# Four-stage sequence model on one core: the turned scores' mask moves from TensorE to VectorE, and two loads of constants move ahead

## Time and profile before

| | |
|---|---|
| median of 3 runs | 4013.48 us (4013.28 to 4015.05) |
| profiled execution | 4030.09 us, its span 4028.3 us |
| busy shares of the span | PE 85%, PEld 58%, DVE 70%, ACT 47%, POOL 22% |
| mean granted clock | 0.936 |
| stage A | about 30 to 899 us of the span |
| stage B begins | 899 us; stage C begins 1785 us |

### The profile page before, as it was taken

The page is one execution under the profiler, slowest core; times in us unless marked ns, Lnnn a source line. Parts: engine busy times, 40 slices in busy tenths (PEclk is TensorE's granted clock), DMA queues, the critical chain, the costliest instruction groups (busy, mean ns, idle before and its releaser), DMA issues.

```text
span 4028.3 us, 71096 instructions
## 1 busy us (share of the span) xinstructions
PE 3416.4 (85%) x28530; PEld 2342.5 (58%) x28530; DVE 2804.6 (70%) x5487; ACT 1889.0 (47%) x3121; POOL 868.1 (22%) x908
## 2 busy tenths in 40 slices
PE   6999999987489888856888888888888888869995
PEld 4555555553255555534566666666666666748774
DVE  4666566555588889856767777777777777647775
ACT  3444444335378787824334444444444443226662
POOL 4000000003312122221122222222222221215553
PEclk7989899898699999978999999999999999969997
DMA  8999300000343434220000000000000000026666
GB/s 293 394 394 372 47 1 2 1 21 24 129 147 119 142 126 137 70 67 1 1 6 7 7 7 7 7 6 7 5 5 7 5 6 7 12 83 230 217 219 184
DMA packets 161497, 354.43 MB, mean 88 GB/s; under 512 B 13821, under 2 KB 98559, under 8 KB 154768
## 3 DMA queue, kind: packets, MB, share of 16 engines
q1 hardware_dynamic: 147088, 324.44, 23.5%
q0 software_dynamic: 14080, 25.45, 1.9%
HBM read 136.82 MB, written 216.67 MB: 88 GB/s over the span
## 4 chain that ended last, share of the span: by engine, by line
PE 54%; DVE 26%; ACT 10%; issue 5%; DMA 2%; SPq 1%; POOL 1%; another core or an unknown queue 0%; DVEq 0%; POOLq 0%; ACTq 0%
DVE t L2185 6%; PE ps L1583 5%; PE ps L134 4%; PE ps L1641 4%; PE ps L136 3%; PE ps L135 3%; DVE t L477 2%; PE ps L1674 2%; PE ps L1680 2%; PE ps L1578 2%; PE ps L333 2%; PE ps L886 2%; ACT t L1025 2%; PE ps L1683 2%; ACT t L1023 2%
## 5 line engine op out<-in xcount | busy, mean ns | idle before, releaser
L2185 DVE COPY_PREDICATED t<-t,ps 128x512 f32<-128x512 uint32 x384 | 349.5, 910 | 130.1 <-PE ps L1641 123.0
L477 DVE TENSOR_REDUCE t<-ps 128x2 f32<-128x512 f32 (+1 forms) x512 | 260.4, 550 | 136.0 <-PE ps L292 135.8
L1960 ACT ACTIVATE t<-ps 128x512 f32<-128x512 f32 (+1 forms) x256 | 138.4, 541 | 441.2 <-PE ps L1683 314.1
L1583 PE MATMUL ps<-t 128*128 128x512 f32 x608 | 312.6, 624 | 23.0 <-DVE t L2051 6.3
L416 ACT ACTIVATE t<-ps 128x768 f32<-128x768 f32 x256 | 207.2, 810 | 265.2 <-PE ps L321 264.5
L134 PE MATMUL ps<-t 128*128 128x512 f32 (+1 forms) x660 | 280.0, 424 | 46.5 <-DVE t L503 26.0
L1674 PE MATMUL ps<-t 128*128 128x128 f32 x1280 | 220.6, 296 | 52.9 <-ACT t L1960 29.7
L136 PE MATMUL ps<-t 128*128 128x512 f32 (+1 forms) x660 | 259.5, 393 | 0.0
L135 PE MATMUL ps<-t 128*128 128x512 f32 (+1 forms) x660 | 259.3, 393 | 0.0
L1674 PEld LDWEIGHTS ps<-t 128*128 128x128 f32 x1280 | 179.0, 194 | 125.3 <-issue 70.3
L1641 PE MATMUL ps<-t 64*128 64x128 f32 x3072 | 228.4, 289 | 25.9 <-DVE t L2157 25.7
(11 more groups left out here) (431 smaller groups left out, 8831.0 us busy)
## 6 DMA issues: line engine op xcount, KB each, us to landing
paired<-t SPq DMA_DIRECT2D x14, 8384.0 KB, 59.5
t<-experts SPq DMA_DIRECT2D x39, 1536.0 KB
sorted<-t SPq DMA_DIRECT2D x22, 1950.0 KB, 8.8
t<-in_wP SPq DMA_DIRECT2D x92, 320.5 KB, 3.5
experts<-t SPq DMA_DIRECT2D x8, 1536.0 KB, 6.1
t<-sorted SPq DMA_DIRECT2D x39, 260.0 KB
t<-answers SPq DMA_DIRECT2D x16, 512.0 KB, 6.6
t<-in_wE SPq DMA_DIRECT2D x8, 768.0 KB, 7.7
```

What stands on the lines that cost most here:

```text
L477: m = dve.e.tensor_reduce(nmf[:, z, blk * 16 + 4 * g + i0:blk * 16 + 4 * g + i0 + 2], ps[:, k:k + 2, a0:a1], AX.X, ALU.max, negate=True)
L1583: pe.e.matmul(ps[out, k, :], lhs, rhs, start=True, stop=True).then_inc(*e_pe(u, name))
L2185: dve.e.copy_predicated(out, msk.bitcast(U32), src).then_inc(*i_dve(k, "lev", li))
```

## The change

Three things change. First, the two mask products behind `p2` go (L321). In their place DVE takes, after ACT's exponential, the minimum of columns 128 to 383 of the slot of `pt` with a float32 tensor `limit` that is 0 at forbidden places and 1e30 elsewhere: the new step `cut(b, j)`, 256 times, one instruction each, in place. Second, `pv` waits for `cut` (signal `allowed`) instead of the exponential. The list of steps places `cut(b-1, j-1)` behind `p2(b-1, j)`, and moves `pv(b-2, 3)` from `j` = 0 to 1, `norm` from 1 to 2, the other `pv` from 2, 4, 6 to 3, 5, 7 and `out` from 3 to 4. The steps `nm_*` and `prep` keep their places. Third, `wB` is asked for in `prepare`, when the experts' weights have been stored, and `wC` late in stage B; to make room the blank rows' source in SBUF is halved, so its transfers go in runs of 4 rows (2,096 B) in place of 8 (4,192 B).

```
 steps_a():
             if b > 0:
                 yield "p2", b - 1, j
-            if b > 1 and j == 0:
+                if j or b > 1:
+                    yield "cut", *((b - 1, j - 1) if j else (b - 2, 7))
+            if b > 1 and j == 1:
                 yield "pv", b - 2, 3
-            if b > 1 and j == 1:
+            if b > 1 and j == 2:
                 yield "norm", b - 2, 0
-            if b > 0 and j in (2, 4, 6):
+            if b > 0 and j in (3, 5, 7):
                 yield "pv", b - 1, j // 2 - 1
-            if b > 1 and j == 3:
+            if b > 1 and j == 4:
                 yield "out", b - 2, 0
...
 stage_a, pe:  p2
-                pe.e.matmul(ps[:, kk, 256:384], ks[r, s, g, o + 128:o + 256], qa[r, z, g, 0:128],
-                            start=False, stop=False, skip_group_check=True)
-            for i in (0, 1):
-                m = pe.e.matmul(ps[:, k + i, 128:384], identb, maskb[:, 1, :],
+                m = pe.e.matmul(ps[:, kk, 256:384], ks[r, s, g, o + 128:o + 256], qa[r, z, g, 0:128],
                                 start=False, stop=True, skip_group_check=True)
...
 pv
-            pe.wait_ge(prob, b, 2 * g + 1)
+            pe.wait_ge(allowed, b, 2 * g + 1)
...
 stage_a, dve
+        dve.e.tensor_scalar(limit[:, 0, :], w["maskk"], -NEG, None, ALU.add).then_inc(*const("limit"))
...
+        def cut(b, j):
+            own = pt[:, (8 * b + j) % SLOTS, :, 128:384]
+            dve.wait_ge(const, "limit")
+            dve.wait_ge(prob, b, j)
+            dve.e.tensor_tensor(own, own, limit.broadcast_to([128, 2, 256]), ALU.min).then_inc(*allowed(b, j))
...
 prepare
-    empty = sb([128, 8 * ROW_B])
+    empty = sb([128, 4 * ROW_B])
...
+        sp.wait_ge(sent[0], 6)
+        sp.wait_ge(sent[1], 7)
+        sp.e.dma_start(c.weights_b, c.aps["wB"]).then_inc(*c.loaded_b())
...
 stage_b, sp
-        sp.e.dma_start(wbuf, c.aps["wB"]).then_inc(*c.loaded("B"))
...
+        sp.wait_ge(three_s, MACROS - 1, 1, 2)
+        sp.wait_ge(gelu, MACROS - 1, 1, "s")
+        sp.e.dma_start(c.weights_c, c.aps["wC"]).then_inc(*c.loaded_c())
         sp.wait_ge(c.emptied, MACROS - 1)
...
 stage_c
-    def sp(sp):
-        sp.wait_ge(c.ended, "B")
-        sp.e.dma_start(wbuf, c.aps["wC"]).then_inc(*c.loaded("C"))
```

More of the change, by code:

```diff
@@ L176, in steps_a @@
             yield from nxt
+    yield "cut", B - 1, 7
     yield "pv", B - 1, 3
@@ L186, in stage_a @@
     w, wbuf = c.weights("A", sb)
-    identb, maskb = sb([128, 128], BF16), sb([128, 2, 256], BF16)
+    identb, maskb = sb([128, 128], BF16), sb([128, 256], BF16)
+    limit = sb([128, 1, 256])
     wr = {n: (sb(list(w[n].shape), F32R), sb(list(w[n].shape), F32R)) for n in ("wq", "wk", "wv")}
@@ L427, in dve @@
         dve.e.tensor_copy(identb, w["ident"])
-        dve.e.tensor_copy(maskb[:, 0, :], w["maskq"])
-        dve.e.tensor_copy(maskb[:, 1, :], w["maskk"]).then_inc(*const("mask"))
+        dve.e.tensor_copy(maskb, w["maskq"]).then_inc(*const("mask"))
+        dve.e.tensor_scalar(limit[:, 0, :], w["maskk"], -NEG, None, ALU.add).then_inc(*const("limit"))
         for n in ("wq", "wk", "wv"):
@@ L527, in out @@
             misc.give(("out", b), out_dve, b, "x")
-        do = dict(load=load, prep=prep, p1=p1, nm_split=nm_split, nm_add=nm_add, norm=norm, out=out)
+        do = dict(load=load, prep=prep, p1=p1, cut=cut, nm_split=nm_split, nm_add=nm_add, norm=norm, out=out)
         for step, i, j in steps_a():
@@ L670, in stage_b @@
     sb = c.tiles(mem)
-    w, wbuf = c.weights("B", sb)
+    w, c.weights_b = c.weights("B", sb)
     w2h = sb([128, 4])
@@ L788, in pe @@
         pe.wait_ge(c.ended, "A")
-        pe.wait_ge(c.loaded, "B")
+        pe.wait_ge(c.loaded_b)
         def read(t):
@@ L942, in act @@
         act.wait_ge(c.ended, "A")
-        act.wait_ge(c.loaded, "B")
+        act.wait_ge(c.loaded_b)
         act.e.preload_act_table_set(NLE)
@@ L1055, in dve @@
         dve.wait_ge(c.ended, "A")
-        dve.wait_ge(c.loaded, "B")
+        dve.wait_ge(c.loaded_b)
         dve.e.tensor_copy(b2[:, 0, :], w["b2"]).then_inc(*w_const("b2hi"))
@@ L1566, in unit_free @@
             e.wait_ge(s_dve, u - 2, "x")
-    def sp(sp):
-        sp.wait_ge(c.ended, "B")
-        sp.e.dma_start(wbuf, c.aps["wC"]).then_inc(*c.loaded("C"))
     def pe(pe):
         pe.wait_ge(c.ended, "B")
-        pe.wait_ge(c.loaded, "C")
+        pe.wait_ge(c.loaded_c)
         def hold(k, n):
@@ L1815, in act @@
         act.wait_ge(c.ended, "B")
-        act.wait_ge(c.loaded, "C")
+        act.wait_ge(c.loaded_c)
         table = [None]
@@ L2026, in dve @@
         dve.wait_ge(c.ended, "B")
-        dve.wait_ge(c.loaded, "C")
+        dve.wait_ge(c.loaded_c)
         dve.e.tensor_scalar(hb, w["ab"], 0.5, None, ALU.mult).then_inc(*hb_s("hb"))
@@ L2402, in pool @@
         pool.e.memset(MT, 0.0).then_inc(*zero("c"))
-        pool.wait_ge(c.loaded, "C")
+        pool.wait_ge(c.loaded_c)
         def feat(u, s):
@@ L2527, in prepare @@
     areas = c.xB[0:PAIRS * AREA, :].rearrange("(n p k) c -> n p (k c)", n=14, p=128)
-    pairs = areas.rearrange("n p (a m) -> n p a m", m=8 * ROW_B)
+    pairs = areas.rearrange("n p (a m) -> n p a m", m=4 * ROW_B)
     rest = c.xB[PAIRS * AREA:ROWS_B, :].rearrange("(p k) c -> p k c", p=128)
@@ L2540, in sp @@
         sp.e.dma_start(dst[7], out[:, 1, :].bitcast(F32)).then_inc(*sent[1](7))
+        sp.wait_ge(sent[0], 6)
+        sp.wait_ge(sent[1], 7)
+        sp.e.dma_start(c.weights_b, c.aps["wB"]).then_inc(*c.loaded_b())
         sp.wait_ge(blank, "row")
         for n in range(14):
-            sp.e.dma_start(pairs[n], empty.rearrange("p (a m) -> p a m", a=1).broadcast_to([128, 16, 8 * ROW_B])
+            sp.e.dma_start(pairs[n], empty.rearrange("p (a m) -> p a m", a=1).broadcast_to([128, 32, 4 * ROW_B])
                            ).then_inc(*c.paired("area", n))
@@ L2929, in _ @@
             for part in parts:
-                part["sp"](engine)
+                if "sp" in part:
+                    part["sp"](engine)
 def stack(parts, layout):
```

8 lines of the change are left out of this document (5 added, 3 removed).

## The result

The changed kernel takes 4210.93 us (median of 4 runs, 4194.74 to 4214.32), the kernel before 4013.38 us beside it: a ratio of 1.0491, 95% interval 1.0468 to 1.0515, about 198 us more. Slower was forecast, but by 121 us, and the time lies 11 us above the upper end of the range. The profiled execution's span is 4209.9 us at a mean granted clock of 0.898 (before 4028.3 and 0.936).

A forecast was written before the change was run, and what follows sets the result against it. PE was taken as stage A's bound, with DVE 275 us free. Fourteen pairs at 6.5 us (waits less saved work) plus 3.3 us low clock gave +137, the loads -16: +121, so 4134 us, range 4036 to 4200.

The forecast's parts named there:

- The mask products and the minimum: Stage A, per two blocks (a pair): PE saves 3.4 us; DVE gains 16 minima of 0.67 us, 10.7 us more.
- The three waits: PE ahead of `mm3`: odd block `j` = 2, 4.8 us; even block `j` = 2 and 3, 3.6; even `j` = 6, 2.6.
- The full-clock pair: Sign of being right: two blocks of stage A take 55 to 56 us at full clock; under 51 would be wrong.
- The clock: Low clock in stage A behind PE's waits: 3.3 us more per pair, bounds -3.3 and +6.6.
- the two longer waits to come: PE's waits of 4.8 us (odd block) and 3.6 us (even block), each charged 3.3 us of low clock.
- the third: PE's wait for `nm_add` at `j` = 6 of even blocks, 2.6 us, charged with no low clock of its own.
- The first rival: Each long wait in stage A sends the clock down, three low stretches of 3.3 us per pair: 4181 us, chance 0.20.
- The other blocks: Four blocks of stage A outside the 14 full pairs: taken as 0, no more than 7 us gained.
- The borders: Waits for `wB` and `wC` at the starts of stages B and C, 7.35 and 8.42 us, vanish: -15.8 us.
- The half-length blank rows: Blank-row transfers of 2,096 B beside stage A run at 314 GB/s, take 383 us, end at about 520: no cost.
- The faster rival: DVE's free time in stage A absorbs the minimum and PE sets the time: -70 us, 3943 us, chance 0.11.

The follow-up runs named there:

- e2: The changed kernel with the two mask products back on PE and no minimum on DVE, new step order and early loads kept: 4187.22 us, ratio 1.0375 to before.
- e3: The changed kernel with 37, 20 and 18 unread products on PE ahead of its three long waits per pair: 4105.73 us, ratio 1.0170 to before.
- e8: The kernel before with the early loads, and `norm` moved to `j` = 2 and `out` to 4, `pv` unmoved: 4126.18 us, ratio 1.0245 to before.
- e1: The kernel before with only the early loads of `wB` and `wC` and the half-length blank rows: 4007.9 us, ratio 0.9942 to before.
- e7: e1 with `norm` moved behind `nm_add` at `j` = 2 in odd blocks alone: 3969.83 us, ratio 0.9858 to before.
- e4: The kernel before's step order with early loads, the mask products replaced by a 0-or-1 product on GpSimd: 4041.2 us, ratio 1.0012 to before.
- e6: e1 with 14 unread products on PE in its one wait of 1.46 us per pair: 3981.16 us, ratio 0.9888 to before.
- e5: The changed kernel with `nm_add` run ahead of `norm` at `j` = 2 on DVE: 4171.75 us, ratio 1.0361 to before.

## Why the prediction was right in direction and wrong in size

**The mask products and the minimum: right.** 681 ns on the row, 0.60 us to the next start, the lower bound. Both together cost +2.4 us per pair (e2 to the changed kernel). The 3.4 us that PE saves were no gain: its waits are 12.0 us per pair where e2's are 8.1 (its two rows and 16.6 us ahead of `p1`, over 13.5 pairs), and the clock fell from 0.85 to 0.78.

**The three waits: right, nearly to the tenth.** Forecast 4.8, 3.6 in two parts and 2.6 us; measured 4.80, 0.74 + 2.83 and 2.58. The chain of the odd block was worked out as 6.90 us from one `mm3` to the next and took 6.81 (557.08 to 563.89); that of the even block as 8.35 and took 8.25 (521.37 to 529.62). In sum 12.0 us of waits per pair, against 2.3 + 9.9 = 12.2 forecast. The full-clock pair was forecast at 55 to 56 us, and e3 shows 55.1. That the order, more than the minimum, makes these waits is what e2 and e8 show.

**The clock: the step that failed.** The prediction charged "the two longer waits to come" with 3.3 us each and the third, which "falls into the second's low stretch", with nothing: 6.6 us of low clock per pair, +3.3 over before. Measured are 65.94 - 55.1 = 10.8 us, +7.5. The third wait does not fall into the second's stretch for free: it has its own in every pair (for one, 0.53 between 608 and 615 us). The first rival had three stretches of 3.3 us, 9.9 per pair, and is the nearer one; its 4181 us fall short mainly for the reason of the next paragraph. It is the one that stood beside the rule of the Trainium skill's "TensorE: Matmul & The Clock Gate", section "Why this matters for your kernels", to leave no long idle gaps between bursts of matmuls. The traces go further than it: the waits of 2.0 to 2.8 us have their low stretch as the one of 4.8 has. e8 agrees in size by an estimate: its full-clock pair would be 49.35 + 0.95 + 2.2 = 52.5 us (the pair of before and what its two waits grew by), so the measured 59.51 holds 7.0 us of low clock for two waits, 3.5 each on the mean. The 4.2 us per pair missing in this term are 4.2 x 13.5 = 57 us, more than the whole 11 us by which the range was left.

**The other blocks: wrong.** "In the other four blocks" 0 was taken. Of stage A's +207.9 us the stretch of 13.5 pairs has 890.17 - 711.01 = 179.2; the other 28.8 lie outside it, where the forecast had half a pair, 4.9. Of these 22.5 stand ahead of the first reciprocal. That one started at 108.3 us before and in e1, at 113.1 in e8, at 125.8 in e2 and at 130.8 in the changed kernel, so the same moves cost there too; about 3 us, a sixteenth of a pair, are only its place one `j` later. The rest looks like the clock again: from 85 us to the reciprocal it is 0.97 before and below 0.6 in the changed kernel, while PE's waits from 35 us on grew by only some 6 us.

**The borders: right.** -7.35 and -8.42 were forecast, -15.1 and -11.2 came, but these are single executions: in the 13 profiles with the early loads stage B takes 870.1 to 884.5 us and what follows 2225.2 to 2247.5, on the mean 7.7 and 4.4 us less than in the one profile of before. So the forecast's size isn't refuted, and that the sum came 10 us lower here is chance as far as is known. No wait for the constants is left. The half-length blank rows cost nothing, as forecast, though the reason given (314 GB/s would do) was too careful.

**The faster rival** needed the waits to grow by less than 4.5 us per pair; they grew by 9.7.

## What to carry to other kernels

When work moves to an engine with free time, look at what stands behind it in that engine's order: here the late places of two unrelated steps cost most, and DVE had a third of its time free throughout. On a kernel that TensorE bounds, count each wait twice, once as itself and once as the low clock behind it, and charge every wait that stands by itself, also the one close behind another. A wait of 1.5 us in front of a busy engine was worth 0.8% of the whole kernel here: a step of two instructions placed behind the one that TensorE waits for (e7), with the early loads, beat both kernels. And work taken from TensorE just ahead of such a wait makes the wait longer (e4).

## What the runs showed of the hardware that was not expected

- Products that nothing reads made a kernel 3.1% faster (e3), and the kernel before with early loads 0.5% faster (e6), by holding the granted clock at 0.96 and 0.99 in stage A in place of 0.78 and 0.94.
- A wait cut from 4.8 to 2.7 us brought back only 0.9 us of low clock per pair besides its own 2.2 (e5). On the mean over its three waits the changed kernel's low clock is 10.8 / 3 = 3.6 us each; in e1 a wait of 1.46 us once per pair goes with 52.22 - 49.35 = 2.9 us on the mean, and some pairs there keep full clock.
- GpSimd's product held up DVE's copies between SBUF tiles. In e4's timeline a copy of 128x16, 0.18 us long otherwise, starts 0.05 us behind a product and ends with it:

```profile
455.22 1.29 POOL L246 TENSOR_TENSOR t<-t 128x512 f32<-128x512 f32 x1 [1.20 <-ACT t L427]
455.27 1.28 DVE L504 COPY t<-t 128x16 f32<-128x16 f32 x1
```

The Trainium skill's "SBUF — State Buffer", section "SBUF: two separate sides", says of some DVE operations, those in a 2-port mode or with two SBUF inputs, that they share a pair of ports with GpSimd, which whoever starts first holds for its whole instruction while the other is blocked; these two rows agree. DVE's reductions, which read PSUM, kept their 550 ns on the mean; the subtraction of two SBUF tiles that makes the normalised input went from 0.69 to 0.98 us, 0.3 of the 0.9 us by which that wait grew in e4.
- Blank rows in runs of 2,096 B went out at 375 GB/s, hardly slower than the 394 of runs twice as long. The forecast had drawn a line between the times of a run of 524 B (145 GB/s) and of 4,192 B, and that gave 314.
